# Seven block products for 448 of 1036 columns per half in two token stages of a quantised-weight FFN kernel on one core

## The reference

```
lora    = lora_B @ lora_A * 0.5                      # 2048 x 2048, rank 64
scaled  = (weight + lora) / exp(scale_log)           # one scale per 128 columns
q       = codebook entry nearest to scaled           # 32 entries, 31 thresholds
w_eff   = q * exp(scale_log) + lora
h       = x @ w_eff.T
ffn(h)  = h @ W_base.T + b_base + mix(h @ A_w.T, softmax(h @ router_w.T), cores) @ B_w.T * 2
out     = x + ffn(h)
```

## Time and profile before

| | |
|---|---|
| median of three runs | 2353.25 us (2351.75 to 2354.31) |
| the profiled execution | 2352.95 us |
| its span, first to last instruction | 2351.2 us |
| TensorE busy | 2281.0 us, 97%, 11,778 matmuls |
| weight loads into TensorE | 2083.8 us, 89% |
| VectorE (DVE) | 1846.1 us, 79% |
| ScalarE (ACT) | 1464.8 us, 62% |
| GpSimd (POOL) | 1288.8 us, 55% |
| data moved | 459.63 MB, 195 GB/s |

### The profile page before, as it was taken

How to read it: one execution, slowest core, us unless ns; L and a number is a source line. 1 busy time by engine, 2 the same in 40 slices (tenths; PEclk the granted TensorE clock), 3 DMA queues, 4 the chain that set the end, 5 groups by cost and what they waited for, 6 DMA issues and landing times.

```text
span 2351.2 us, 31846 instructions
## 1 busy us (share of the span) xinstructions
PE 2281.0 (97%) x11778; PEld 2083.8 (89%) x11778; DVE 1846.1 (79%) x2363; ACT 1464.8 (62%) x1926; POOL 1288.8 (55%) x792
## 2 busy tenths in 40 slices
PE   3989899999999999999999999999999999999999
PEld 2445479999999989999999989999999999999998
...
PEclk9999999999999999999999999999999999999999
...
GB/s 210 262 284 280 312 199 164 164 176 136 145 134 133 116 98 190 230 240 226 221 243 149 115 102 162 227 232 228 241 204 208 186 195 202 206 200 235 189 225 153
DMA packets 133088, 459.63 MB, mean 195 GB/s; under 512 B 14098, under 2 KB 66898, under 8 KB 96082
## 3 DMA queue, kind: packets, MB, share of 16 engines
...
HBM read 306.41 MB, written 151.13 MB: 195 GB/s over the span
## 4 chain that ended last, share of the span: by engine, by line
PE 91%; DVE 6%; ACT 2%; DMA 1%; issue 1%; DVEq 0%; SPq 0%; ACTq 0%
PE m L970 15%; PE m L969 15%; PE m L971 15%; PE m L926 5%; PE m L927 5%; PE m L925 5%; PE m L868 5%; DVE acc L1362 4%; PE m L1018 4%; PE m L1020 4%; PE m L1019 4%; PE m L956 2%; PE m L957 2%; PE m L958 2%; ACT mk L1131 1%; PE pd L1018 1%
## 5 line engine op out<-in xcount | busy, mean ns | idle before, releaser
L1362 DVE SCALAR_TENSOR_TENSOR acc<-mk,dj,acc 128x1024 f32<-128x1024 uint8 x736 | 945.4, 1285 | 102.8 <-ACT mk L1131 83.6
L1131 ACT ACTIVATE mk<-wr,bj 128x1024 uint8<-128x1024 f32 x736 | 809.0, 1139 | 1.0 <-DVE acc L1362 0.5
L970 PE MATMUL m<-gl,xh 128*128 128x384 f32 (+2 forms) x1920 | 674.1, 351 | 0.0
L969 PE MATMUL m<-gh,xh 128*128 128x384 f32 (+2 forms) x1920 | 673.5, 351 | 0.0
L971 PE MATMUL m<-gh,xl 128*128 128x384 f32 (+2 forms) x1920 | 671.6, 350 | 0.0
L1606 POOL TENSOR_TENSOR pp<-pp,tm 128x1024 f32<-128x1024 f32 x184 | 447.3, 2431 | 22.3 <-POOL tm L1592 0.6
L971 PEld LDWEIGHTS m<-gh,xl 128*128 128x128 f32 x1920 | 360.6, 188 | 18.0
L969 PEld LDWEIGHTS m<-gh,xh 128*128 128x128 f32 x1920 | 361.0, 188 | 17.2
L970 PEld LDWEIGHTS m<-gl,xh 128*128 128x128 f32 x1920 | 360.9, 188 | 16.9
L1592 POOL TENSOR_SCALAR tm<-mp,dj 128x1024 f32<-128x1024 uint8 x192 | 217.6, 1134 | 281.5 <-ACT mp L1137 276.3
L1413 DVE TENSOR_TENSOR kl<-kw,kh 128x416 fp32r<-128x416 f32 (+3 forms) x310 | 238.0, 779 | 104.9 <-ACT kh L1165 103.7
...
## 6 DMA issues: line engine op xcount, KB each, us to landing
...
kw<-in_ws SPq DMA_DIRECT2D x128, 208.0 KB, 2.6
...
```

The lines of the kernel that those rows point to most:

```text
L969: e.matmul(R.m[c][:, 0:w], xh, gh, start=k == 0, stop=False)
L970: e.matmul(R.m[c][:, 0:w], xh, gl, start=False, stop=False)
L1131: e.activation(R.mk[m % NM], w, ACT.Identity, bias=R.bj[:, j:j + 1], scale=GROW).then_inc(S["mk"], 1)
L1362: e.scalar_tensor_tensor(R.acc, R.mk[m % NM], R.dj[:, j:j + 1], R.acc, ALU.mult, ALU.add).then_inc(S["ac"], 1)
```

## The change

The token stages of groups 1 and 2 are rewritten. Pairs 0 and 15 of the 16 pairs of tokens stay as they were. In the 14 pairs between, the first SW = 448 columns of each half of the row are computed with the seven block products, and the remaining 588 columns of each half as before, in three pieces of REST = 392 columns a token (the third made of the last 196 columns of each half). That is 13 units a pair (`MIX`) in place of ten chunks: a product is 2 x 3 matmuls of 448 columns in banks 0 and 1, a rest is 4 x 3 matmuls of 392 in the other four banks.

- `spread` (VectorE, once a stage, in the first pair) adds high and low parts of G back together and forms the four sums of G's blocks, eight operations of 896 columns; `spread_high` (ScalarE) and `spread_low` (GpSimd) round them. They lie in the buffers of the rounded weights `wh`.
- `token_sums` (GpSimd) forms the four sums of each pair's x blocks one pair ahead, with `token_sums_high` (ScalarE) and `token_sums_low` (GpSimd). They, and a fourth x buffer, lie in raw weight buffers that are free (`SPARE_RAW`).
- As the sums use the `wh` buffers, the eight halves of a group are split in the last, unmixed pair (`SPLITS`), in an order that gives the first four for slots 0 to 7 and the others for slots 8 on; of the last group four wait until slots 20 to 32 of the last weights stage (`LATE_SPLITS`).
- Half 24, whose raw buffer holds a part of the sums, is loaded and normalised at the close of group 1's token stage.
- `ON_SCALAR`: in halves 18 to 23 and 26 to 31 ScalarE scales the spare levels' masks (all but the first), and GpSimd only adds them.
- The memset of `bw` and `cr` moves from the end of group 2's token stage to slot 4 of the last weights stage.
- The store of a token's partial sum waits for its last unit, and the loads of the next ones are issued at the pair's fifth and tenth unit.

```diff
+ON_SCALAR = tuple(range(18, 24)) + tuple(range(26, 32))
...
+SW = 448
+REST = (HX - SW) // 3 * 2
+MIX = (("prod", 1), ("prod", 2), ("rest", 0, 0), ("prod", 6), ("rest", 0, 1), ("prod", 5), ("rest", 0, 2), ("prod", 7),
+       ("prod", 3), ("rest", 1, 0), ("prod", 4), ("rest", 1, 1), ("rest", 1, 2))
+MIXED = (1, 2)
+MIX_FIRST, MIX_LAST = 1, PAIRS - 2
+NMIX = MIX_LAST - MIX_FIRST + 1
+SUM_SLOT = {4: 0, 6: 1, 5: 2, 3: 3}
+SPARE_RAW = {1: (3, 4, 2), 2: (0, 1, 10)}
+SPLITS = {1: tuple(range(8, 16)), 2: (16, 18, 20, 22, 17, 19, 21, 23), 3: (24, 26, 25, 27, 28, 29, 30, 31)}
+SPLIT_POS = {q: 8 * (g - 1) + k for g, qs in SPLITS.items() for k, q in enumerate(qs)}
+LATE_SPLITS = {20: 28, 24: 29, 28: 30, 32: 31}
...
+def mixed_tokens_of(g, back):
+    until = UNTIL_TOKENS[g]
+    back.begin(until)
+    costs = [unit_columns(u) for u in UNITS_OF[g]]
+    total, passed = sum(costs) - 7 * NCH * width(0), 0
+    for k, u in enumerate(UNITS_OF[g]):
+        p, at = u[0], k - PAIR_FIRST[g][u[0]]
+        yield ("mul", g, k)
+        if at == 0:
+            yield ("fetch", g, p)
+        if p == 0 and at in (0, 1, 2):
+            yield ("spread", g, at)
+        if p == 0 and at in (1, 2, 3, 4):
+            yield ("spread_high", g, at - 1)
+            yield ("spread_low", g, at - 1)
+        if p + 1 < PAIRS:
+            if at == 3:
+                yield ("x_split", g, 2 * p + 2)
+            if at == 4:
+                yield ("x_split", g, 2 * p + 3)
+                yield ("more", g, p)
+            if at == 5 and mixed(p + 1):
+                yield ("token_sums", g, p + 1)
+            if at == 6:
+                yield ("x_low", g, 2 * p + 2)
+            if at == 7:
+                yield ("x_low", g, 2 * p + 3)
+            if at == 9 and mixed(p + 1):
+                yield ("token_sums_high", g, p + 1)
+                yield ("token_sums_low", g, p + 1)
+        elif at < 8:
+            if g + 1 < LAST or at < 4:
+                yield ("split", SPLITS[g + 1][at])
+        if at == (9 if mixed(p) else 5):
+            yield ("half_done", g, p)
+        if p == PAIRS - 1 and at == 6:
+            yield ("next_weights", g)
+        if p == PAIRS - 1 and at == 8:
+            yield ("next_rounded", g)
+        passed += costs[k]
+        yield from back.levels(until, min(1.0, passed / total), 0)
+    yield ("close", g)
...
+        if s == 4:
+            yield ("cleared",)
+        if s in LATE_SPLITS:
+            yield ("split", LATE_SPLITS[s])
...
+        if q == 2 * FIRST[LAST]:
+            e.wait_ge(S["mc"], sums_free(1))
...
-            if j == 0 and 2 * N0 < q + 1 < NQ:
+            if j == 0 and 2 * N0 < q + 1 < NQ and q + 1 != 2 * FIRST[LAST]:
...
+        elif what == "fetch":
+            g, p = at
+            if p + 1 < PAIRS:
+                load_x(g, 2 * p + 2)
+                load_x(g, 2 * p + 3)
+            if p:
+                store_part(g, 2 * p - 1)
+        elif what == "more":
+            g, p = at
+            if p:
+                load_part(g, 2 * p + 2)
+        elif what == "half_done":
+            g, p = at
+            store_part(g, 2 * p)
+            if p + 1 < PAIRS:
+                load_part(g, 2 * p + 3)
+        elif what == "next_weights":
+            for s in range(RING):
+                weight(at[0] + 1, s)
         elif what == "close":
             if at[0] + 1 < LAST:
                 store_part(at[0], NT - 1)
+            if at[0] == 1:
+                raw(2 * FIRST[LAST])
...
-            e.wait_ge(S["wl"], 2 * FIRST[g + 1] - 2 * N0)
+            e.wait_ge(S["wl"], 8 * g if g == 1 else 8 * g - 4)
+        if s == 8:
+            e.wait_ge(S["wl"], 8 * g)
...
+    def mul(g, k):
+        p, kind, *at = UNITS_OF[g][k]
+        if kind == "chunk":
+            t, c = 2 * p + at[0], at[1]
+            if c == 0:
+                e.wait_ge(S["xl"], NT * g + t + 1)
+            ready(g, t, c)
+        elif k == PAIR_FIRST[g][p]:
+            e.wait_ge(S["xl"], NT * g + 2 * p + 1)
+        elif (kind, *at) == ("rest", 1, 0):
+            e.wait_ge(S["xl"], NT * g + 2 * p + 2)
+        if (kind, *at) == ("prod", 6):
+            e.wait_ge(S["ql"], sums_count(g, p))
+            e.wait_ge(S["bl"], 4 * g)
+        before = bank_before(g, k)
+        if before is not None:
+            e.wait_ge(S["ed"], added(g, before))
+        if kind == "chunk":
+            product(g, t, c, True).then_inc(S["mc"], 1)
+            return
+        bank = (*R.m, R.pd)[unit_bank(UNITS_OF[g][k])]
+        if kind == "prod":
+            n = at[0]
+            for kp in range(2):
+                high, low = sum_factor(g, p, n, kp)
+                oh, ol = sum_operand(n, kp, False), sum_operand(n, kp, True)
+                e.matmul(bank[:, 0:SW], high, oh, start=kp == 0 and n in (1, 2, 5), stop=False, skip_group_check=n in (3, 4, 6, 7))
+                e.matmul(bank[:, 0:SW], high, ol, start=False, stop=False, skip_group_check=n in (3, 4, 6, 7))
+                done = e.matmul(bank[:, 0:SW], low, oh, start=False, stop=kp == 1, skip_group_check=n in (3, 4, 6, 7))
+        else:
+            u, i = at
+            _, xl, xh = R.token(g, 2 * p + u)
+            for b in range(GROUP[g]):
+                r = slice(b * 128, (b + 1) * 128)
+                gh, gl = rest_columns(R.gh[b], i), rest_columns(R.gl[b], i)
+                e.matmul(rest_bank(bank, i), xh[:, r], gh, start=b == 0, stop=False)
+                e.matmul(rest_bank(bank, i), xh[:, r], gl, start=False, stop=False)
+                done = e.matmul(rest_bank(bank, i), xl[:, r], gh, start=False, stop=b == GROUP[g] - 1)
+        done.then_inc(S["mc"], 1)
...
+            if q in ON_SCALAR and i:
+                e.wait_ge(S["mp"], k + 1)
+                e.wait_ge(S["tm"], k)
+                e.wait_ge(S["pp"], NA * q + i - 1)
+                e.activation(R.tm[0], R.mp[k % 2], ACT.Identity, bias=0.0,
+                             scale=R.dj[:, NV + i:NV + i + 1]).then_inc(S["tm"], 1)
...
+    def spread_high(g, k):
+        e.wait_ge(S["br"], 8 * (g - 1) + (3, 5, 6, 8)[k])
+        e.activation(R.sum_h[k], R.sum_f[k], ACT.Copy).then_inc(S["bh"], 1)
+    def token_sums_high(g, p):
+        e.wait_ge(S["qs"], 4 * sums_count(g, p))
+        if p > MIX_FIRST:
+            e.wait_ge(S["mc"], multiplied(g, prod_unit(g, p - 1, 3)))
+        elif g > 1:
+            e.wait_ge(S["used"], NS * g)
+        e.activation(R.sh[g], R.sf, ACT.Copy).then_inc(S["qh"], 1)
...
+    def mul_added(g, k):
+        p, kind, *at = UNITS_OF[g][k]
+        t = 2 * p + unit_tokens(UNITS_OF[g][k])[0][0]
+        part, bank = R.part[t % 3], (*R.m, R.pd)[unit_bank(UNITS_OF[g][k])]
+        if k == first_unit(g, t, 0):
+            e.wait_ge(S[f"pi{t % 3}"], slot_round(g - 1, t))
+        e.wait_ge(S["mc"], multiplied(g, k))
+        if kind == "chunk":
+            c = at[1]
+            to, of = part[:, cols(c)], bank[:, 0:width(c)]
+        elif kind == "rest":
+            to, of = rest_columns(part, at[1]), rest_bank(bank, at[1])
+        else:
+            first = HX * TARGET[at[0]][1]
+            to, of = part[:, first:first + SW], bank[:, 0:SW]
+            before = target_before(g, k)
+            if before is not None:
+                e.wait_ge(S["ed"], added(g, before))
+        e.tensor_tensor(to, of, to, ALU.add).then_inc(S["ed"], 1)
+    def spread(g, k):
+        br, r, f, n = S["br"], R.sum_raw, R.sum_f, 8 * (g - 1)
+        def rebuilt(to, i, h):
+            e.tensor_tensor(grouped(r[to], 2), both_blocks(R.gah, i, h).bitcast(F32), both_blocks(R.gal, i, h).bitcast(F32),
+                            ALU.add).then_inc(br, 1)
+        if k == 0:
+            e.wait_ge(S["used"], NS * g)
+            e.wait_ge(S["lo"], NCH * FIRST[g + 1])
+            rebuilt(1, 0, 1)
+            rebuilt(0, 0, 0)
+            e.wait_ge(br, n + 2)
+            e.tensor_tensor(f[0], r[1], r[0], ALU.subtract).then_inc(br, 1)
+        elif k == 1:
+            rebuilt(2, 1, 1)
+            e.wait_ge(br, n + 4)
+            e.tensor_tensor(f[1], r[2], r[1], ALU.subtract).then_inc(br, 1)
+            e.tensor_tensor(f[2], r[2], f[0], ALU.subtract).then_inc(br, 1)
+        else:
+            rebuilt(3, 1, 0)
+            e.wait_ge(br, n + 7)
+            e.tensor_tensor(f[3], r[3], f[2], ALU.subtract).then_inc(br, 1)
...
+        elif what == "cleared":
             wait_consumed(e, S, RAW * (NQ // RAW) + 1)
+            e.wait_ge(S["mc"], MC_BASE[LAST])
...
+    def spread_low(g, k):
+        e.wait_ge(S["bh"], 4 * (g - 1) + k + 1)
+        if k in (0, 2):
+            e.wait_ge(S["br"], 8 * (g - 1) + (6 if k == 0 else 8))
+        e.tensor_tensor(R.sum_l[k], R.sum_f[k], R.sum_h[k].bitcast(F32), ALU.subtract).then_inc(S["bl"], 1)
+    def token_sums(g, p):
+        n, x = 4 * (sums_count(g, p) - 1), [R.token(g, t)[0] for t in (2 * p, 2 * p + 1)]
+        a11, a12, a21, a22 = (quarter(x[k // 2], 0, k % 2) for k in range(4))
```

(19 more changed lines are left out.)

205 lines of the change are left out of this document (169 added, 36 removed), and 1 row of the table COMPUTE.

## The result

The changed kernel takes **2382.84 us** (median of 4 runs, 2381.81 to 2384.93) where the kernel before took 2352.5 in the same measurement (4 runs, 2351.63 to 2354.31): a ratio of 1.0129, 95% interval 1.0112 to 1.0147. It is 30 us slower. I had forecast 2347 and a range that ended at 2363, so both the sign and the range were wrong.

The account below looks back on a forecast made before the run. The prediction took TensorE's matmul columns as the bound (91% of the chain, upper clock level throughout); -34.2 + 18 + 6.5 + 3 + 1 = -5.7 us from 2352.95 gave 2347 us, range 2331 to 2363.

Parts of the forecast that it names:

- The columns: Mixed pairs of both token stages: 2,688 fewer matmul columns a pair at an unchanged pace, -34.2 us over 28 pairs.
- The start of each mixed stage: Second pair: TensorE waits for GpSimd's queue, mainly the token sums' low part; 9 us each, +18 (4 to 21).
- Half 24: Group 2's weights stage: raw load and normalising now come after group 1's token stage, TensorE waits +6.5 us (5 to 9).
- The splits of the other stages move into the last pair ... nothing.: Last unmixed pair: GpSimd's eight splits make 19 of its 22.6 us, four wanted only 17 us later; no cost.
- The steady pairs: Mid-stage mixed pairs: VectorE's adds fit between products with 1.4 us to spare; 1.5 us a stage, +3 (0 to 20).
- the 10 that I had named as a sign of being wrong: Mid-stage: the prediction was to count as failed if TensorE's steady waits passed 10 us.
- the second rival: Mixed pairs: VectorE becomes the bound, mask waits doubled to 28 us; 21 us instead of 3, 2365 us; chance 0.22.
- The last weights stage: Memset of bw and four rounded weights now lie inside it, with 3.4 us of cover; +1 us (0 to 4).
- partial sums that arrive late: Mixed pairs: a rival with transfers landing as slowly as now, up to 1 us a pair, 28 in all, 2370; chance 0.04.

Follow-up runs that it names:

- the base of three: Changed kernel with two unmixed pairs in front, group 1's last split behind the next stage's first rounded weights, and half 24 loaded as before the change: 2353.57 us, ratio 1.0002.
- the last run: Kernel before, TensorE made to wait at six token starts in groups 1 and 2 until the previous token's partial sum is stored: 2428.79 us, ratio 1.0326.

## Why the prediction was wrong, step by step

- **The columns, -34.2.** Right. Matmuls of 448 and 392 columns keep the pace, and the account above closes with it to half a microsecond.
- **The start of each mixed stage, +18 for two.** Right in size and cause: the six waits (for an add, x low and the sums' low part: 2.5, 1.9 and 4.5 us in group 1; 2.5, 1.9 and 5.8 in group 2) are 19.2 us. GpSimd's first spread low came 10.4 us after the stage's first matmul, with 9.5 worked out as the earliest; the sums' low part was done at 38.4, with 35.2 to 37.5 worked out. What I did not put behind it was the lower clock (1.6, 1.5 and 2.5 us) and that VectorE and GpSimd go into the steady pairs behind time. Two plain pairs in front gave back 20 us.
- **Half 24, +6.5.** Its wait was 4.3 us in the changed kernel and 6.7 once nothing else stood in front of the load. Right.
- **"The splits of the other stages move into the last pair ... nothing."** This step failed. I had weighed GpSimd's time against TensorE's need and not asked what stands in ScalarE's queue behind the last split while its input isn't there. It stood 9.7 us, with the first weights of the next stage, the last adds, the last store and the load of half 24 behind it: 5.3 us of TensorE and 2.6 of clock.
- **The steady pairs, +3.** This step failed by size: 12.6 us of waits in mid-stage, past the 10 that I had named as a sign of being wrong, and some 4 us of clock behind them. It is the second rival's mechanism (masks late since ScalarE's spare time is halved: 47 us of idle time in front of the levels against the 28 that it assumed), at less than its price of 21. I had looked at ScalarE's spare time on the average and not at where its queue stands. The runs show both: on the base of three, the waits for the adds fall from 14.2 to 4.3 us with the x work two units later and the same work on every engine, and to 4.9 with less work on ScalarE and the same order.
- **The last weights stage, +1.** The waits there are 5.3 us, about 4 over the kernel before. At the upper bound; one of them, at 1944 us, has 1.5 us of clock behind it.
- **What had no term at all: the clock.** This step failed. I read the tenths of the earlier trace rows as the upper level throughout, and kept that level for a stream into which my own sum put several stops. The earlier trace rows do show 1.00, but for stages in which TensorE never stops; a slice of the page is 59 us long and hides a stretch of a few us, and the first stage of the kernel before has six, the one shown above behind a stop of 2.8 us. So a row that prices a stop was in the trace before the change, outside the windows of the earlier trace rows. The lower clock cost 17 us, more than half of the 30. The six stops of the last run price it at 2.0 to 2.3 us for a stop of 10, and the changed kernel at 1.3 to 2.6 for those of 1.8 to 5.8 that have it.

By terms, the miss of the profiled execution (2384.93 against 2347.2, so 37.7 us; by the medians 35.8 over 2347): clock 17, steady waits 10, splits 5, last stage 3, starts, half 24 and what each stop costs beyond its wait about 3. The forecasts for the starts, the columns and half 24 stand. The rivals covered only one of the two large misses, so the range could not reach. One rival's own sum was off: partial sums that arrive late, at 28 us more, come to 2375 and not 2370. No such wait appeared.

What stays open: why stops of 1.7 to 2.5 us are followed by the lower clock in some places (1013.77, 1578.80, 1616.31) and not in others (908.09, 1226.64, 1472.32); no run was made for it. Their length does not decide it: the first stop of group 1's stage is 2.52 us long in the changed kernel and in the one with half 24 loaded as before, with the same work around it, and the clock behind it is 1.00 in the one (ended at 908.09) and 0.50 in the other (907.53). So one stretch more or less, some 1.5 us, need not come from what an edit is about. And the gain of 13 us from the later x work is shown only on the base of three edits; in the changed kernel I have no edit that removes the mid-stage waits without paying at the starts.
